# Absolute values and exponentials of the step sizes, chunk by chunk in turns in place of two passes

## The reference, cut to what matters

```python
ts, Bm, Cm = ssm[..., :R], ssm[..., R:R + N], ssm[..., R + N:]   # R = 32, N = 16
ts, Bm, Cm = rms_forward(ts), rms_forward(Bm), rms_forward(Cm)
dt = softplus(ts @ W_dt.T + b_dt)                                # 1024 channels x 512 steps
A = -exp(A_log)
# then for each step: state = state * exp(dt * A) + (dt * u) * B;  y = state . C
```

## Time and profile before

| | us |
|---|---|
| three runs | 2827.97, 2830.35, 2831.92 |
| median | 2830.35 |
| profiled execution, own time | 2823.24 |
| its span from first to last instruction | 2821.4 |
| mean granted TensorE clock | 0.961 |

### The profile page before, as it was taken

One profiled execution on the slowest core, in us unless ns is written; L12 is line 12 of the kernel. 1 busy time (PEld: TensorE's weight loads), 2 busy tenths in 40 slices (PEclk: granted clock), 3 DMA queues, 4 the chain that ended last, 5 costly groups with the idle time before them and its releaser, 6 DMA issues. The chain is left out here.

```text
span 2821.4 us, 43498 instructions
## 1 busy us (share of the span) xinstructions
PE 2617.2 (93%) x17272; PEld 2397.5 (85%) x17272; DVE 1918.0 (68%) x2192; ACT 1526.1 (54%) x2706; POOL 1483.3 (53%) x1005
## 2 busy tenths in 40 slices
PE   7999999999999999999999999997876886897788
PEld 6899999999999999999999999996763335775667
DVE  2266776677667767776777677665558997887773
ACT  3455665566556655665566556654345442664652
POOL 2354754655564574474475465530018980685652
PEclk9999999999999999999999999998988997998879
DMA  5310111110111011011111010014221003441100
GB/s 203 135 47 24 61 47 31 46 62 24 34 47 57 25 52 57 28 54 47 38 47 54 24 61 23 31 34 175 83 90 73 0 1 112 130 151 46 50 1 15
DMA packets 90414, 163.79 MB, mean 58 GB/s; under 512 B 8114, under 2 KB 57522, under 8 KB 87658
## 3 DMA queue, kind: packets, MB, share of 16 engines
q1 hardware_dynamic: 81898, 152.70, 16.2%
q10 hardware_dynamic: 8320, 8.39, 0.9%
HBM read 143.17 MB, written 17.89 MB: 57 GB/s over the span
## 5 line engine op out<-in xcount | busy, mean ns | idle before, releaser
L357 POOL TENSOR_TENSOR xa_pt_lo<-xa_st,xa_pt_hi 128x1024 fp32r<-128x1024 f32 x255 | 509.2, 2030 | 595.7 <-ACT xa_pt_hi L543 595.7
L54 PE MATMUL xa_kv_ps<-ctx_wv_hi,ctx_hi 128*128 128x256 f32 (+1 forms) x1664 | 467.6, 281 | 3.1 <-DVE xa_v_lo L634 3.1
L56 PE MATMUL xa_kv_ps<-ctx_wv_hi,ctx_lo 128*128 128x256 f32 (+1 forms) x1664 | 469.8, 282 | 0.0
L55 PE MATMUL xa_kv_ps<-ctx_wv_lo,ctx_hi 128*128 128x256 f32 (+1 forms) x1664 | 465.3, 280 | 0.0
L54 PE MATMUL xa_kv_ps<-ctx_hi,ctx_wk_hi 128*128 128x402 f32 (+1 forms) x1024 | 356.5, 348 | 2.7 <-DVEq L711 2.2
L56 PE MATMUL xa_kv_ps<-ctx_hi,ctx_wk_lo 128*128 128x402 f32 (+1 forms) x1024 | 353.1, 345 | 0.0
L55 PE MATMUL xa_kv_ps<-ctx_lo,ctx_wk_hi 128*128 128x402 f32 (+1 forms) x1024 | 352.8, 345 | 0.0
L634 DVE TENSOR_TENSOR xa_v_lo<-xa_kv_ps,xa_v_hi 128x512 fp32r<-128x512 f32 (+1 forms) x224 | 146.2, 653 | 265.7 <-ACT xa_v_hi L516 264.7
L54 PEld LDWEIGHTS xa_kv_ps<-ctx_wv_hi,ctx_hi 128*128 128x128 f32 (+1 forms) x1664 | 306.5, 184 | 3.3 <-DVE xa_v_lo L634 3.3
L55 PEld LDWEIGHTS xa_kv_ps<-ctx_wv_lo,ctx_hi 128*128 128x128 f32 (+1 forms) x1664 | 308.5, 185 | 0.0
L56 PEld LDWEIGHTS xa_kv_ps<-ctx_wv_hi,ctx_lo 128*128 128x128 f32 (+1 forms) x1664 | 306.7, 184 | 0.0
(11 more groups left out here) (415 smaller groups left out, 7040.4 us busy)
## 6 DMA issues: line engine op xcount, KB each, us to landing
ca_nat<-in_ctx SPq DMA_DIRECT2D x48, 512.0 KB, 4.0
ctx_raw<-in_ctx_t SPq DMA_DIRECT2D x24, 804.0 KB, 6.6
ctx_wk_raw<-in_xa_wk SPq DMA_DIRECT2D x64, 256.0 KB, 2.8
ctx_wv_raw<-in_xa_wv SPq DMA_DIRECT2D x32, 512.0 KB, 4.3
q_raw<-in_xa_wq SPq DMA_DIRECT2D x8, 1024.0 KB, 4.9
q_scratch<-q_q_sb ACTq DMA_DIRECT2D x8, 1024.0 KB, 4.4
xa_q_raw<-q_scratch SPq DMA_DIRECT2D x64, 128.0 KB, 2.6
o_scratch<-xa_o_sb SPq DMA_DIRECT2D x64, 128.0 KB, 1.7
```

Source lines behind the costliest of these rows:

```text
L54: nc.tensor.matmul(out, left[0], right[0], start=first, stop=False)
L55: nc.tensor.matmul(out, left[0], right[1], start=False, stop=False)
L56: return nc.tensor.matmul(out, left[1], right[0], start=False, stop=last)
L357: nc.gpsimd.tensor_tensor(by_chunk(pt_lo, p), scored(j, p).rearrange("p g q c -> p g c q"), by_chunk(pt_hi, p).bitcast(F32), ALU.subtract) ...
```

## The change

ACT's first two passes become one loop. In it the exponential of chunk c - 1 follows the absolute value of chunk c; the last exponential stands alone behind the loop. The pass of logarithms, the semaphores, their counts and all other engines' code stay as they are.

```diff
+            def decline(c):
+                act.wait_ge(d_abs, c + 1)
+                nc.scalar.activation(dt_sb[:, c, :], dt_sb[:, c, :], ACT.Exp, scale=-1.0).then_inc(e_set, 1)
+
             for c in range(DC):
                 act.wait_ge(d_full, c + 1)
                 nc.scalar.activation(dt_sb[:, c, :], d_ps[:, c % 4, :], ACT.Abs, bias=bd[:, c:c + 1]).then_inc(d_abs, 1)
-            for c in range(DC):
-                act.wait_ge(d_abs, c + 1)
-                nc.scalar.activation(dt_sb[:, c, :], dt_sb[:, c, :], ACT.Exp, scale=-1.0).then_inc(e_set, 1)
+                if c > 0:
+                    decline(c - 1)
+            decline(DC - 1)
             for c in range(DC):
                 act.wait_ge(e_set, c + 1)
                 nc.scalar.activation(dt_sb[:, c, :], dt_sb[:, c, :], ACT.Ln, bias=1.0).then_inc(ln_set, 1)
```

## The result

| | kernel before | changed kernel |
|---|---|---|
| median of ten runs, us | 2828.84 | 2822.48 |
| lowest and highest, us | 2825.52, 2833.98 | 2817.48, 2827.43 |
| profiled execution: own time, us | 2823.24 | 2827.43 |
| profiled execution: span, us | 2821.4 | 2825.6 |

The account below looks back on a forecast made before the run. The stage was bounded by PE's eight chunks, then ACT's load, exponentials, load and first logarithm, then DVE's additions and the barrier. One load and six exponentials hidden under PE's pace gave 2830.35 - 4.56 = 2825.8 us, range 2821.5 to 2829.5.

Parts of the forecast that it names:

- Front half led by PE, back half by ACT: Changed stage: PE's eight chunks, one every 1.44 us, set the front; ACT then works alone on exponentials and logarithms.
- The load: Table load for exponentials, moved behind the second absolute value: 1.30 us with its pauses, slipped into ACT's waits for PE.
- The turn: One absolute value and one exponential on ACT: 1.11 to 1.30 us, under PE's 1.44.
- Absolute value 2 late by 1.07, waits for PE at chunks 6 and 7: ACT's loop: the load delays chunk 2 by 1.07 us; ACT gains 0.33 per chunk and catches up by chunk 6.
- PE not held up: PE's chunk 6 needs the bank read after the late absolute value 2: 1.6 us of slack, costed at nothing.
- 4.56 us from the stage: ACT reaches the second load, before the logarithms, at 2116.04 instead of 2120.60; 3.91 us earlier at the slower turn.
- Sums unchanged under the broadcasts: DVE's eight additions stay at 7.05 us though broadcasts cover most of them; 0.06 us as the other end.
- Passed on in full: The stage's gain reaches the kernel's end, the scan moving as a whole: profiled span 2816.8 us.
- Under what can be told: Whole kernel: 0.16% faster, below the 0.2% (5.66 us) a measurement can tell from no change.
- clock luck: Rival, stages behind the scan: TensorE's clock stays high longer, 1.2 us or more extra gain, about 2823 us; chance 0.20.
- The pause: Rival, ACT's new loop: an extra 1.28 us pause or a slow turn; gain 2.6 us, time 2827.7; chance 0.12.
- Reloads at every turn: Rival, ACT's new loop: table changes every turn, 3.87 us a turn, 11.4 us later, time 2841.8; chance 0.01.

Follow-up runs that it names:

- early load: Kernel before plus a one-column exponential that loads the exponentials' table before chunk 0; 24.9 us from chunk 0 to the scan's memset, ratio 0.9997.
- same chunk: Changed kernel with the early load, and exponential c behind absolute value c instead of c + 1; 21.4 us from chunk 0, ratio 0.9984.
- 200 copies: Changed kernel plus two hundred unused ScalarE copies between last exponential and logarithms' load; 125.6 us from chunk 0, ratio 1.0354 against before.
- nine copies: Changed kernel plus nine unused ScalarE copies between last exponential and logarithms' load; 26.5 us from chunk 0, ratio 1.0004 against before.
- repeated kernel: The changed kernel run and traced again, nothing edited; 2821.04 us, ratio 0.9984 against the kernel before.
- first comparison: First ten runs of the changed kernel against the kernel before; 2822.48 us, ratio 0.9976.
- both: Changed kernel plus the early load; 21.8 us from chunk 0, ratio 0.9985 against the kernel before.

## Why the prediction was right

- *Front half led by PE, back half by ACT.* As said. With the early load added nothing more came, so with this order PE's chunk 7 is the limit.
- *The load.* Put at 1.30 us, from the end of absolute value 1 to exponential 0: 2110.69 to 2112.00, 1.31.
- *The turn.* Bounded by 1.11 and 1.30, taken at 1.11; it is 1.09 (2112.54 to 2113.63). The overlap of 0.10 us, taken from one pair of other operations in the earlier trace rows, held (absolute value 7 at 2118.64, exponential at 2119.23: 0.59). It holds only for an operation that doesn't need the one just before: in the same chunk order it is gone.
- *Absolute value 2 late by 1.07, waits for PE at chunks 6 and 7.* Late by 1.10 (2112.54 for the 2111.44 that PE's 1.44 us give); four waits, chunks 0, 1, 6 and 7.
- *PE not held up.* Chunk 7 comes 10.01 us after chunk 0, before 10.02.
- *4.56 us from the stage.* 4.54 in the first trace and as much in the second. Two experiments split it as the prediction did: 1.4 us for the load, 0.5 for each of six exponentials.
- *Sums unchanged under the broadcasts.* 7.05 us both times; the other end of 0.06 us wasn't needed.
- *Passed on in full.* The 200 copies show it to within a twentieth, and the nine copies took the gain away again (1.0004). The profiled span of 2816.8 us was missed (2825.6): front + 4.3, scan + 2.8, behind + 1.6. A single span is no test of 4.5 us. The repeated kernel's span, 2817.3, lies close by luck: its front is 2.6 us longer than in the first trace of before, its scan 0.3, and the rest 2.4 shorter.
- *The time.* 2825.8 us was forecast from a median of three runs; 2822.48 is 3.3 less. 1.5 of that is the median of before, which is 2828.84 over ten runs, and 1.8 is what the medians differ by beyond 4.56. That the time lay in the range owes something to the range's width, 8 us for a gain of 4.56. Its ends follow their own sums only to 0.3 us (2825.8 - 4 is 2821.8, and half of 4 over 2827.7 is 2829.7), which decides nothing.
- *Under what can be told.* The chances were 0.76 on "within 0.2%" and 0.20 on "faster". The first comparison gave 0.9976, the second 0.9984 (0.9976 by its medians), so the value sits near the line, where the draw decides the name. The rival "clock luck" is neither shown nor excluded: the clock's effect in the scan of the first trace is a loss of 2.8 us, and what the stages behind the scan do differs by up to 7.3 us from trace to trace. Why the first comparison came out 2.3 us beyond the stage's gain stays open; the spread of runs is enough for it. The rival's price took a matmul at 1.00 for half of one at 0.50; by the rows of the scan it is 3.70 for 6.61, so its 11.3 us are nearer to 10, an estimate from these two rows.
- *The pause.* Refuted: in every trace shown a load takes 1.28 us and its function starts 1.29 or 1.30 after the load's start. The Trainium skill's page "ScalarE: Activation LUTs", section "What ACT_TABLE_LOAD costs", adds 1380 ns of drain to each; with the table changing at every turn, 16 times 1380 ns would be 22 us more, an estimate by that page. The trace has none of it: 39.3 us were measured and 39.4 expected without a drain. (The prediction's sum by the page, a gain of "3.6 to 2.6 us", should begin at 3.8: with 1.36 us more, chunk 7 is late by 0.78 at 1.11 us a turn.)
- *Reloads at every turn.* The order excluded it for the change. The rival, priced at 11.4 us, had absolute value and exponential change the table; what was run has exponential and logarithm do so, and costs 12.9. It shows the price of a load at every turn, not that rival itself.

What the prediction lacked: it named the clock behind the scan as the place of luck or loss, and called the scan a block that moves as a whole. The scan has a place of its own where the clock counts, 15 to 22 us in, when matmuls stand ahead of those that make the inputs of a step.

## What to carry to other kernels

When one engine waits for another at an even pace and later runs alone, fill its waits with its later work on chunks that are there. The floor is the last chunk's arrival plus what must follow it, and here a load and six of eight exponentials, 4.5 us, slipped under. Working one chunk behind makes a turn shorter (1.09 us) but leaves two exponentials for the end. Where the turn fits into the other engine's pace even with the wait for a direct predecessor, as it does here with the table loaded early, taking the same chunk leaves only one, and the stage was 0.4 us shorter. Check in the built order that the functions share a table, since each change cost 1.3 us here. Where a gain is as small as the spread of runs, measure the stage instead of the whole, and ask a large filling whether the stage's time reaches the end.

## What was not expected of the hardware

- TensorE's granted clock, back at 1.00 after 8 to 9 us of work at 0.50, fell again in 7 of 7 such traces, for 3 to 7 us: at 38 to 39 us into the scan after a rise at 8, at 15 to 16 after a rise at 9. Where it came back after 13 or 14 us it fell in one of six. The scan's code is the same in all. The fall at 15 or 16 went with a scan up to 3.3 us longer, of which 2.9 us in the first trace are eight matmuls that took 6.61 us for 3.70.
- An activation of 128 x 512 that needs the result of the one just before started 0.03 us after its end ("same chunk", absolute value at 2118.12, exponential at 2118.84); one that doesn't, 0.10 before it ("both", 2117.19 and 2117.78).
- VectorE's sum of 128 x 512 beside a GpSimd product took 1.76 us, without one 0.68; two products of 1.65 to 1.71 us on GpSimd cost VectorE 2.2 us, and two done by VectorE itself 1.2.
